# One more doubled quad of chunk 7, and two pairs of the third chunk moved up to the turn

## What is computed

```
def _ggc(x, adj, W, wih, whh, bih, bhh):
    m = adj @ (x @ W)
    gi = m @ wih.T + bih
    gh = x @ whh.T + bhh
    ...
    return (1.0 - z) * n + z * x
h = relu(_ggc(x, adj, W1, ...)); x = layernorm(x + relu(_ggc(h, adj, W2, ...)))
support = x @ weight
mask = (adj != 0); rank = cumsum(mask, axis=1); k = minimum(deg, 100)
w = mask * where(pos > 0, 0.5 ** (k - pos), 0)      # pos = rank - (deg - k)
x = layernorm(x + w @ support + bias)
```

## Time and profile before

| | before |
|---|---|
| median of 3 runs | 356.19 us (355.62 to 356.23) |
| profiled execution, its time | 355.52 us |
| its span in the trace | 353.8 us |
| PE busy | 333.5 us, 94% |
| DVE busy | 302.6 us, 86% |
| ACT busy | 180.3 us, 51% |
| matrix transfers | 204 of 512 KB |
| granted clock of PE | 0.995 |

### The profile page before, as it was taken

The page is one execution under the profiler, slowest core; times in us unless marked ns, Lnnn a source line. Parts: engine busy times, 40 slices in busy tenths (PEclk is TensorE's granted clock), DMA queues, the critical chain, the costliest instruction groups (busy, mean ns, idle before and its releaser), DMA issues.

```text
span 353.8 us, 6689 instructions
## 1 busy us (share of the span) xinstructions
PE 333.5 (94%) x2496; PEld 155.2 (44%) x2496; DVE 302.6 (86%) x510; ACT 180.3 (51%) x235; POOL 24.8 (7%) x32
## 2 busy tenths in 40 slices
PE   1998999999999999999999989999999999989992
PEld 1342333333333333333333324544444445869992
DVE  0689879898999999987985658899899999888996
ACT  0202404123041230367466438877896969676993
POOL 2000000000000000000000001202020202022044
PEclk9999999999999999999999999999999999999997
DMA  7999999999999999999898999989999996000002
GB/s 251 414 408 410 409 408 409 408 409 395 400 360 327 401 348 368 343 355 340 283 345 296 372 409 408 378 317 342 348 384 368 386 384 233 17 3 2 4 32 90
DMA packets 32720, 111.10 MB, mean 314 GB/s; under 512 B 3632, under 2 KB 6192, under 8 KB 32688
## 3 DMA queue, kind: packets, MB, share of 16 engines
q1 hardware_dynamic: 31824, 109.20, 81.1%
q10 hardware_dynamic: 864, 1.48, 1.1%
HBM read 109.62 MB, written 1.05 MB: 313 GB/s over the span
## 4 chain that ended last, share of the span: by engine, by line
PE 82%; DMA 10%; DVE 4%; issue 1%; ACT 1%; POOL 1%; POOLq 0%; ACTq 0%; DVEq 0%
PE m_acc L446 43%; PE out L446 15%; DMA stream<-in_adj_t 8%; PE out L558 7%; PE gate_ps L506 4%; PE gate_ps L558 3%; PE gate_ps L513 3%; PE gate_ps L529 2%; PE m_acc L558 2%; DMA w<-in_w 2%; PE gate_ps L438 1%; PE m_acc L478 1%; POOL rstd L846 1%; DVE stream L1158 0%; PE out L490 0%
## 5 line engine op out<-in xcount | busy, mean ns | idle before, releaser
L446 PE MATMUL m_acc<-stream,s_in 128*64 128x512 f32 x512 | 125.7, 604 | 2.6 <-DMA stream<-in_adj_t 1.9
L906 DVE TENSOR_SCALAR codes<-stream 128x1024 uint8<-128x1024 f32 x117 | 76.8, 686 | 4.8 <-DMA stream<-in_adj_t 4.6
L446 PE MATMUL out<-stream,s_mid 128*64 128x512 f32 x272 | 69.1, 595 | 1.1 <-DMA stream<-in_adj_t 1.0
L446 PEld LDWEIGHTS m_acc<-stream,s_in 128*64 128x64 f32 x512 | 34.3, 138 | 68.3 <-issue 52.6
L446 PE MATMUL m_acc<-stream,s_mid 128*64 128x512 f32 x240 | 53.9, 597 | 0.0
L846 POOL TENSOR_TENSOR rstd<-var,mhalf 128x4 f32<-128x4 f32 x16 | 22.9, 1434 | 325.3 <-DVE var L1061 325.3
L955 DVE SCALAR_TENSOR_TENSOR codes<-codes,run 128x384 uint32<-128x384 uint32 (+2 forms) x56 | 43.0, 768 | 1.9
L950 DVE TENSOR_TENSOR run<-run,codes 128x768 uint16<-128x768 uint16 (+2 forms) x55 | 41.5, 755 | 1.8
L641 ACT ACTIVATE m_high<-m_acc 64x512 f32<-64x512 f32 x13 | 7.7, 593 | 59.1 <-PE m_acc L446 45.7
L446 PEld LDWEIGHTS out<-stream,s_mid 128*64 128x64 f32 x272 | 19.2, 137 | 39.8 <-issue 39.3
L673 ACT ACTIVATE rz<-gate_ps,b_rz 128x256 f32<-128x256 f32 x32 | 13.4, 467 | 43.9 <-PE gate_ps L513 43.9
(11 more groups left out here) (139 smaller groups left out, 378.3 us busy)
## 6 DMA issues: line engine op xcount, KB each, us to landing
stream<-in_adj_t SPq DMA_DIRECT2D x204, 512.0 KB, 6.3
x_res<-in_x_pairs SPq DMA_DIRECT2D x8, 128.0 KB, 6.9
out_nodes<-stream SPq DMA_DIRECT2D x8, 128.0 KB, 2.0
hx<-in_x_pairs ACTq DMA_DIRECT2D x1, 512.0 KB, 7.4
const<-in_consts ACTq DMA_DIRECT2D x1, 358.0 KB, 6.9
hx<-in_x_pairs ACTq DMA_DIRECT2D x2, 128.0 KB, 6.0
hx<-in_x_pairs ACTq DMA_DIRECT2D x1, 256.0 KB, 8.8
bias_b<-in_bias SPq DMA_DIRECT2D x1, 128.0 KB, 4.9
```

The costliest lines, as they stand in the source:

```text
L446: last = nc.tensor.matmul(to[D * u:D * (u + 1), :], state[:, t * D:(t + 1) * D], stream[:, n % SLOTS, u * CW:(u + 1) * CW], start=start[u] ...
L906: nc.vector.tensor_scalar(edges(p // 2, b, 2 * (p % 2), 2), stream[:, n % SLOTS, :], 0.0, None, ALU.not_equal).then_inc(mask_made, 1)
```

## The change

Chunk 7 now has 7 doubled quads, numbered through `TRI[7] = 7`: pairs 0 to 13, so only 14 and 15 are single, and they take places 2 and 5 in the order of the chunk, where 12 and 13 stood. Pairs 12 and 13 come third from last and last, since the state for their columns is made in the course of chunk 7. Pass 2 loads them no more: 202 transfers in place of 204. In the turn, (0, 12) and (0, 13) fall away and (2, 12) and (2, 13) of step 2 come in; the turn still has 12 products. Stage 1 has 7 pairs in place of 8 and stage 6 has 10 in place of 11; the other stages keep their number, but each of their lists begins one pair later in its step.

```
-TRI = (0, 1, 2, 3, 4, 5, 5, 6)
+TRI = (0, 1, 2, 3, 4, 5, 5, 7)
...
-    [[0, 12, 1, 2, 13, 3, 6, 7, 4, 14, 5, 8, 9, 10, 15, 11]]
+    [[0, 14, 1, 2, 15, 3, 8, 9, 4, 10, 5, 6, 7, 12, 11, 13]]
...
-    [(slice(0, 2), slice(3, 7, 3), slice(2, 5, 2), slice(5, 8, 2))]
+    [(slice(0, 2), slice(4, 8, 3), slice(2, 4), slice(5, 7))]
...
-TURN = [(0, 12), (0, 13), (1, 10), (1, 11), (1, 12), (1, 13), (2, 10), (0, 14), (0, 15),
-        (1, 14), (1, 15), (2, 11)]
+TURN = [(1, 10), (1, 11), (1, 12), (1, 13), (2, 10), (2, 11), (2, 12), (0, 14), (0, 15),
+        (1, 14), (1, 15), (2, 13)]
...
-ALONG_PAIRS = {1: 8, 2: 10, 3: 12, 4: 12, 5: 11, 6: 11}
+ALONG_PAIRS = {1: 7, 2: 10, 3: 12, 4: 12, 5: 11, 6: 10}
...
-RES_AT = [FIRST[1], *(n + SLOTS + 3 for n in FIRST[1:NCH - 1]), len(LOADS)]
+RES_AT = [FIRST[1], *(min(n + SLOTS + 3, len(LOADS) - 1) for n in FIRST[1:NCH - 1]), len(LOADS)]
```

## The result

The changed kernel takes 358.38 us (median of 4 runs, 357.85 to 359.48), against 356.19 before (4 runs, 355.62 to 356.23): 2.19 us more, a ratio of 1.0078 with a 95% interval of 1.0059 to 1.0096. A second comparison (the last experiment) gave 357.87 against 355.71: 2.16 more, 1.0068 (1.0046 to 1.0091). The profiled execution took 357.85 us with a span of 356.1, so 2.33 more than that of before.

The account below looks back on a forecast made before the run. PE, then DVE's chain from gates(7) to gates(9), then PE to node(12), then DVE bound the kernel; +0.87 (turn) + 1.00 (node) - 0.32 (slack) + 0.36 (put-backs) = +1.9, so 358.1 us, range 356.3 to 359.0.

Parts of the forecast that it names:

- Step 1: Pass 1: two more pair products on PE, with no idle time to hide them, make gates(7) 1.72 us later.
- Step 2: The turn: gates(8) comes right behind combine(8), +0.87 us, with the transfer waits gone and the twelfth load's landing unchanged.
- my other end: The turn, latest case: the twelfth load lands 1.72 us later too, and gates(8) is +1.72.
- Step 3: Stage 1: one pair and one transfer less gain nothing, since gates(9) waits for x1s; gates(9) +0.87, PE idle some 1.4 us.
- Step 4: Put-backs ahead of node: in stage 2 node(9) loses 1.00 us more; DVE's slack of 0.32 leaves +1.55 at stage 3's t_n.
- Step 5: Stages 3 and 4: put-backs wait for combine(11) and combine(12), 0.33 and 0.73 us, making PE +1.20, then +1.9.
- Step 6: Stage 5 to the end: node(12) keeps +1.9 us (0.36 from put-backs behind combine); stage 6's missing pair gains nothing.

Follow-up runs that it names:

- the last experiment: The changed kernel unaltered, run again beside the kernel before: 357.87 us against 355.71, ratio 1.0068.
- experiment 4: The changed kernel with 8 pairs in stage 1 in place of 7 and 9 in stage 6 in place of 10: 359.40 us, ratio 1.0094.
- experiment 6: The changed kernel with node and the shares after three pairs, ahead of the put-back, in stage 2 alone: 357.65 us, ratio 1.0050 to the kernel before.
- experiment 5: The changed kernel with node and the shares after 3 pairs in place of 4 in stages 2 to 4: 360.55 us, ratio 1.0119.
- experiment 2: The changed kernel with 6 pairs in stage 1 and 11 in stage 6, in place of 7 and 10: 356.78 us against 355.49 before.
- 3: The kernel before with the last pair of stage 1 moved to stage 2 (7 and 11 pairs): 356.52 us against 355.84.
- 7: The kernel before with loads 130 to 147 (most of turn and stage 1) moving only half their bytes: 354.93 us against 355.49.
- experiment 11: The kernel before with one pair moved from stage 4 to stage 6: 355.10 us against 355.71, ratio 0.9983.

## Why the prediction was right, and by how much each step was off

The forecast was +1.9 us and the measurement +2.2, with the mechanism as told: the turn, node in stage 2, the put-back behind combine in stages 3 and 4. By its steps, in the profiled execution:

**Step 1** said gates(7) +1.72; it is +1.72.

**Step 2** said gates(8) +0.87, with no transfer waited for. It is +1.06. combine(8) came exactly as said (207.43 + 0.68 = 208.11), and the weight loads with it, but the last product of the turn was not done: it waited for its transfer. The chain of waits shows the landing:

```profile
201.05 6.38 DMA stream<-in_adj_t
207.42 0.14 issue
207.56 1.08 PE out L446 x4
```

It landed at 207.42, where I had taken it as unchanged near 206.4. That is the term that failed: I had let the transfers use the spare room between 190 and 197, 115 GB/s over 7 us. They used 10 of it: 304 GB/s after against 294 before. A load is issued when a slot comes free, so PE's pace ahead of the turn holds it back. In the trace of the changed kernel the loads leave at 188.06, 189.78, 191.50 and 193.22, each 1.72 us after the last, the time of a pair's two products; 524 KB in 1.72 us is 305 GB/s. Spare bandwidth in a stretch is of no use to loads that aren't issued in it.

The error was 0.19 here and 0.46 in the second execution, and that it was so small is in part luck. Six profiled executions have this same turn. In them gates(8) stands 0.06, 0.33, 0.35, 0.60, 0.82 and 0.91 behind the end of combine(8) (experiment 4, changed, 6, changed again, 5, 2), where I had 0.14. Experiment 4 shows the turn as I forecast it, without a wait for a transfer:

```profile
202.40 5.70 PE L446 MATMUL out<-stream,s_mid 128*64 128x512 f32 x24
```

and experiment 2 is near my other end: gates(7) is +1.95 and gates(8) +1.86. So the turn costs between 0.8 and 1.9 us by the execution; by medians it is 0.93 (2.19 less the 1.26 behind gates(8)) to 1.29 (experiment 2).

**Step 3** said that gates(9) keeps its distance from gates(8) and that the missing pair is worth nothing. gates(9) is +1.07 with 1.08 idle (I said some 1.4); experiments 2, 3 and 7 bear it out, with the exceptions told in experiment 11.

**Step 4** said that node(9) loses 1.00 on gates(9). It loses 1.15 (+2.22 against +1.07). The chain of waits, from the first pairs of stage 2 to node(9):

```profile
222.85 2.73 PE m_acc L446 x12
225.57 1.00 PE m_acc L478 x2
226.57 1.01 PE m_acc L446 x4
227.58 0.65 PE gate_ps L529 x8
```

2.73 + 1.00 + 1.01 = 4.74, where the kernel with put-backs behind node (experiment 2) has 3.58 for its four pairs. Of the 1.16, 1.00 is the put-back and 0.16 the break that it makes in the row of pairs: a pair takes 0.86 if a pair follows and 1.01 if a put-back or node does. Before, the put-back stood right behind the shares and made no break of its own. The row of 1.00 that I read the earlier trace rows was right and not the whole price; the same 0.15 stays in PE's own row (gates(10) is +1.22), where I had the total of the stage as unchanged. DVE's slack of 0.32 at t_n of stage 3 was 0.33.

**Step 5** said waits of 0.33 and 0.73; they are 0.18 and 0.55. combine(11) and combine(12) came 0.33 and 0.35 later than I had said, by the errors of steps 2 and 4, but PE came later still, by 0.44 and 0.48: gates(10) and gates(11) were 0.35 and 0.39 later than I had them, and a row of three pairs has a length of 2.79 in the trace where I took the distance of 2.70. That t_n of stage 4 passes all of its delay on, its idle 0.63 being ACT's, holds: +1.89, with 0.64 idle. Its cost was told as a wait. Experiment 6 shows that it is the place of the put-back and node(11) behind combine(12), with the wait only the sign of it.

**Step 6** said 0.36 beyond that; it is 0.95 at DVE's sum in stage 4, less 0.42 at t_n of stage 5 (the figure that I had worked out) and 0.09 at the sum behind it, so 0.44. (My "some 2.4 late" for DVE out of stage 4 had no working behind it; it left with 2.84.) At that sum it is again PE that is last: ACT's square waits for node(12), and DVE for the square (0.08). ACT, before and after:

```profile
276.80 0.38 ACT L716 ACTIVATE sq<-gate_ps 128x256 f32<-128x256 f32 x1 [0.59 <-PE gate_ps L529]
```

```profile
279.13 0.39 ACT L716 ACTIVATE sq<-gate_ps 128x256 f32<-128x256 f32 x1 [0.49 <-PE gate_ps L529]
```

PE's row alone gives the same total: gates(9) +1.07, then 0.15, 0.37 and 0.74 in stages 2, 3 and 4, so +2.33 at gates(12) and node(12), for my 0.87 + 0.33 + 0.70. From there DVE carries +2.33 to the end unchanged. Stage 6's missing pair did nothing: gates(14) is only +1.47 on PE and node(14) waits for DVE all the same.

In sum 1.06 + 1.15 - 0.33 + 0.44 = 2.32, for 0.87 + 1.00 - 0.32 + 0.36 = 1.9. The three small errors, 0.19, 0.15 and 0.08, have one direction.

What stays open: why the waits of the turn and of stage 1 differ between executions (gates(8) at +1.06 and +1.90 for the changed kernel), and why gates(7) is later than +1.72 in some of them (+2.29 above). What more slots would bring was not tried either.

## What to carry to other kernels

Ask of every instruction that a change moves not what it costs but who stands behind it on its engine and which slower chain waits for that one; four products of 1 us, moved ahead of node, cost 1 us of the kernel because node stood behind them. A work item taken out of a stage whose end another engine sets is worth nothing there and costs its full length where it goes; look for the stage in which the engine itself is last, as the one pair from stage 4 to 6 suggests (0.6 us by medians). And count spare bandwidth only for transfers that are issued in time to use it.

## What the runs showed of the hardware

A break in a row of equal products on PE costs 0.15 us: the pair ahead of a put-back or of node takes 1.01 in place of 0.86, before and after alike. In stages 3 and 4 of both kernels, seven slots carried eight pairs in a row behind the shares without a wait, and not nine (experiment 5), where the last waited 0.89 and 1.30 us. That is no fixed number: in stage 5 of experiment 6 two of seven waited, 0.16 and 0.19. When PE lives from hand to mouth on transfers, pairs come 1.26 to 1.28 us apart (210.04, 211.30, 212.58), which is 524 KB at some 410 GB/s, and each shows a wait of only 0.18 to 0.20: a short wait can stand for 0.4 us lost, so distances between starts say more than the idle time in brackets.
